# A macaron block with routed experts: the zero fill of the slot table in three large transfers, and matmuls in TensorE's waits

## The reference, cut to what matters

```python
def ffn(x):                               # 16 experts, 2 per token, one shared expert
    probs = softmax(x @ Wr.T + bias)      # (1024, 16)
    val, idx = top_k(probs, 2)
    w = val / (sum(val) + 1e-9)
    y_e = (silu(x @ Wg[e]) * (x @ Wu[e])) @ Wd[e]       # 256 -> 128 -> 256
    routed = sum over the 2 chosen e of w * y_e
    shared = (silu(x @ sWg) * (x @ sWu)) @ sWd
    return routed + shared

def attention(x):                         # 16 heads of 16
    S[i, j] = K[i] . Q[j] * 16 ** -0.5,  -inf for j > i,  decay -(i - j)
    return (softmax(S) @ V) @ o_w.T + o_b

x = x + 0.5 * ffn(layernorm(x))
x = x + attention(layernorm(x))
x = x + 0.5 * ffn(layernorm(x))
```

## Time and profile before

| | |
|---|---|
| median of 3 runs | 366.13 us (365.73 to 367.26) |
| the profiled execution | 365.38 us |
| its span, first to last instruction | 363.6 us |
| mean granted TensorE clock | 0.838 |
| busy share of the span | PE 70%, DVE 70%, ACT 44%, POOL 38% |

### The profile page before, as it was taken

How to read it: one execution, slowest core, us unless ns; L and a number is a source line. 1 busy time by engine, 2 the same in 40 slices (tenths; PEclk the granted TensorE clock), 3 DMA queues, 4 the chain that set the end, 5 groups by cost and what they waited for, 6 DMA issues and landing times.

```text
span 363.6 us, 6430 instructions
## 1 busy us (share of the span) xinstructions
PE 255.2 (70%) x1856; PEld 194.3 (53%) x1856; DVE 254.5 (70%) x839; ACT 160.9 (44%) x411; POOL 136.6 (38%) x212
## 2 busy tenths in 40 slices
PE   1713562999991289679899989898619419999910
PEld 1512551999980169324344444466418309999800
DVE  5673498588883987798688888556676406888716
ACT  3344671455553145315465666756142104656500
POOL 7003884288886014272000000000007732888830
PEclk9966595799997569955999999999867957999965
DMA  5999963655502405863333322000002243555127
GB/s 171 269 182 344 336 237 113 220 157 156 168 23 66 166 0 154 244 183 77 89 87 89 83 52 46 1 2 0 3 0 72 104 134 112 167 154 174 39 78 268
DMA packets 33871, 45.63 MB, mean 125 GB/s; under 512 B 5869, under 2 KB 27419, under 8 KB 33838
## 3 DMA queue, kind: packets, MB, share of 16 engines
q1 hardware_dynamic: 29246, 36.25, 35.4%
q0 software_dynamic: 4592, 8.98, 7.3%
HBM read 27.99 MB, written 20.61 MB: 134 GB/s over the span
## 4 chain that ended last, share of the span: by engine, by line
PE 30%; DMA 19%; POOL 17%; DVE 11%; issue 10%; SPq 8%; ACT 3%; POOLq 0%; DVEq 0%
PE bank L299 18%; POOL slots_x L513 9%; DMA slots_x<-zeros 7%; POOL results L527 6%; DMA stk_q<-parts_d 6%; SPq L412 5%; DVE bank L1261 3%; PE bank L873 3%; PE bank L824 3%; DMA yg<-results 2%; PE bank L886 2%; DMA slots_x<-xn,slot 2%; PE bank L734 2%; POOL yi L521 1%; PE bank L910 1%
## 5 line engine op out<-in xcount | busy, mean ns | idle before, releaser
L527 POOL DMA_INDIRECT results<-ysb,yi x62 | 61.0, 984 | 27.6 <-DVE ysb L1166 14.2
L1261 DVE CUSTOM_DVE_ANT_0 bank<-bank,dec 128x512 f32<-128x512 f32 (+3 forms) x128 | 59.9, 512 | 13.2 <-PE bank L873 12.7
L707 ACT ACTIVATE ct<-bank 128x512 f32<-128x512 f32 (+1 forms) x96 | 46.1, 528 | 39.7 <-PE bank L890 39.1
L513 POOL DMA_INDIRECT slots_x<-xn,slot x32 | 35.5, 1111 | 42.0 <-DMA slots_x<-zeros 19.4
L873 PE MATMUL bank<-stk_q,stk_k 96*128 96x512 bf16 (+3 forms) x128 | 38.6, 343 | 9.1 <-DMA stk_q<-parts_d 4.6
L1127 DVE TENSOR_TENSOR hm<-sg,bank 128x128 f32<-128x128 f32 x78 | 22.3, 287 | 29.7 <-ACT sg L586 29.7
L299 PE MATMUL bank<-wh,xT_h 128*128 x124 | 41.9, 338 | 1.2 <-DVE xT_l L1154 1.2
L624 ACT ACTIVATE xT_h<-bank 128x256 fp32r<-128x256 f32 x62 | 23.8, 384 | 35.8 <-PE bank L824 35.1
L586 ACT ACTIVATE sg<-bank 128x128 f32<-128x128 f32 x78 | 21.6, 276 | 40.2 <-PE bank L299 40.1
L505 POOL COPY xn<-to_row 128x4 int32<-128x4 int32 x8 | 2.4, 301 | 94.0 <-DVE xn L1045 94.0
L824 PE MATMUL bank<-ident,xb 128*128 128x128 f32 x124 | 25.3, 292 | 17.7 <-DMA xb<-slots_x 17.3
(11 more groups left out here) (174 smaller groups left out, 685.9 us busy)
## 6 DMA issues: line engine op xcount, KB each, us to landing
xb<-slots_x SPq DMA_DIRECT2D x62, 128.5 KB
w_raw<-in_experts SPq DMA_DIRECT2D x17, 384.0 KB, 13.5
yg<-results SPq DMA_DIRECT2D x16, 256.0 KB, 4.8
slots_x<-zeros SPq DMA_DIRECT2D x1, 3983.5 KB, 25.6
parts_d<-part SPq DMA_DIRECT2D x6, 384.0 KB, 3.2
stk_k<-parts_d SPq DMA_DIRECT2D x8, 192.0 KB, 3.4
stk_q<-parts_d SPq DMA_DIRECT2D x8, 192.0 KB, 3.7
res<-in_x SPq DMA_DIRECT2D x4, 256.0 KB, 3.5
```

The lines of the kernel that those rows point to most:

```text
L513: pool.indirect_dma_start(slots_x, where, xn[:, t, :], None)\
L527: pool.indirect_dma_start(results, where, ysb[c % RING][:], None, bounds_check=4 * N - 1, oob_is_err=False).then_inc(s_ys[c % RING], 16)
L707: act.activation(ct[n % 6][:, a:b], bank[2 + i][:, 0:b - a], ACT.Exp).then_inc(s_exp, 1)
L1261: dve.tensor_tensor_reduce(s_i, s_i, dec[:, SEQ - w:SEQ], 1.0, NEG, ALU.add, ALU.max, mmax[g % 2][:, n % G * QT + i:n % G * QT + i + 1])\
```

## The change

Four things change.

1. The fill. `zeros` has 11 rows a partition instead of one, and lies in the memory that later holds the `ct` tiles. VectorE writes it as its first work (before: POOL). SP fills the table in three transfers of 11, 10 and 10 rows a partition. The loads of qk_b, v_b and o_b move behind the fill, the shared expert's load stays ahead of it, and r_b and the constant `eps` have semaphores of their own. POOL's scaling of q's bias moves behind the first scatters.
2. The first logits. `logits(0, 0)` runs between the second and third group of transposes and `logits(0, 1)` between the third and the fourth; VectorE's low half of the router weights comes two steps earlier.
3. `keep_busy`: bfloat16 matmuls of 512 columns into a bank whose content isn't used then. Six before the blocks of each `ffn`, when the last group of scatters has landed; seven when the first results have been loaded ahead of attention, and four after each of its first two groups of transposes; four before each of the last two groups of transposes ahead of the second routing.
4. Waits: the scatter waits for three transfers instead of one.

```diff
+        sb("below_zeros", [P, 2 * KT * N], F32, r6)
+        zeros = sb("zeros", [P, 11, XW], F32, r6)
-        zeros = sb("zeros", [P, XW], F32, r2)
...
             sp.dma_start(rw_s[:], r_w).then_inc(s_rws, 16)
-            sp.dma_start(rb[:], r_b.partition_broadcast(P)).then_inc(s_small, 16)
+            sp.dma_start(rb[:], r_b.partition_broadcast(P)).then_inc(s_rb, 16)
+            load_expert(0)
+            rows_of = slots_x.rearrange("(p a) d -> p a d", p=P)
+            sp.wait_ge(s_zero, 2)
+            for a, n in ((0, 11), (11, 10), (21, 10)):
+                sp.dma_start(rows_of[:, a:a + n, :], zeros[:, 0:n, :]).then_inc(s_fill, 16)
             sp.dma_start(qkb[:], qk_b).then_inc(s_small, 16)
             sp.dma_start(vb[:], v_b.partition_broadcast(P)).then_inc(s_small, 16)
             sp.dma_start(ob[:], o_b.partition_broadcast(P)).then_inc(s_small, 16)
-            load_expert(0)
-            sp.wait_ge(s_zero, 3)
-            sp.dma_start(slots_x.rearrange("(p a) d -> p a d", p=P),
-                         zeros[:, None, :].to_broadcast([P, NB, XW])).then_inc(s_fill, 16)
...
-            pool.memset(eps[:], EPS_LN).then_inc(s_zero, 1)
-            pool.memset(zeros[:, 0:D], 0.0).then_inc(s_zero, 1)
-            pool.memset(zeros[:, D:XW].bitcast(I32), NOWHERE).then_inc(s_zero, 1)
+            pool.memset(eps[:], EPS_LN).then_inc(s_eps, 1)
...
-                            pool.wait_ge(s_fill, 16)
+                            pool.wait_ge(s_fill, 48)
...
-            pool.wait_ge(s_small, 64)
+            scatter(0)
+            pool.wait_ge(s_small, 48)
             pool.tensor_scalar(qkb[:, 0, :], qkb[:, 0, :], HD ** -0.5, None, ALU.mult).then_inc(s_qkb, 1)
-            scatter(0)
...
+            def keep_busy(to, n):
+                for _ in range(n):
+                    pe.matmul(to[:], ident_b[:], below_b[:, None, :].to_broadcast([P, QT, P]), start=True, stop=True,
+                              skip_group_check=True)
...
                 pe.wait_ge(s_bex, f + 1)
+                pe.wait_ge(s_sc[3], 8 * NT * (f + 1))
+                keep_busy(bank[5], 6)
...
-            for r in range(NP_):
+            for r in range(2):
                 pe.wait_ge(s_xn, r + 1)
                 turn(0, r)
+            pe.wait_ge(s_const, 2)
             pe.wait_ge(s_rw, 2)
-            pe.wait_ge(s_const, 2)
-            for r in range(NP_):
+            logits(0, 0)
+            pe.wait_ge(s_xn, 3)
+            turn(0, 2)
+            logits(0, 1)
+            pe.wait_ge(s_xn, 4)
+            turn(0, 3)
+            for r in (2, 3):
                 logits(0, r)
...
+            pe.wait_ge(s_yg[0], 16)
+            keep_busy(bank[5], 7)
             for r in range(2):
                 pe.wait_ge(s_xn, NP_ + r + 1)
                 turn(1, r)
+                keep_busy(bank[5], 4)
...
             for r in (2, 3):
+                keep_busy(bank[7], 4)
                 pe.wait_ge(s_xn, 2 * NP_ + r + 1)
                 turn(3, r)
...
-                    dve.wait_ge(s_small, 64)
+                    dve.wait_ge(s_rb, 16)
...
+            dve.memset(zeros[:, :, 0:D], 0.0).then_inc(s_zero, 1)
+            dve.memset(zeros[:, :, D:XW].bitcast(I32), NOWHERE).then_inc(s_zero, 1)
             for r in range(NP_ + 2):
...
-                if r == NP_:
-                    router_low()
                 if r >= 2:
                     turn_low(0, r - 2)
+                if r == 2:
+                    router_low()
```

6 lines of the change are left out of this document (5 added, 1 removed).

## The result

| | median | runs | profiled execution | its span | mean clock |
|---|---|---|---|---|---|
| before | 366.56 us | 365.73 to 367.26 | 365.38 | 363.6 | 0.838 |
| after | 352.69 us | 350.94 to 357.05 | 350.94 | 348.8 | 0.876 |

The ratio is 0.9644, with a 95% interval of 0.9583 to 0.9705: 13.1 us faster, where 5.4 were forecast. Disturbed executions are left out of all ratios here.

What follows compares the result with a forecast made beforehand. The slow zero fill, then scatters beside VectorE's splits, bound the start; TensorE's low clock costs later stretches. 365.38 - 3.3 - 0.6 - 1.1 - 0.4 = 360.0, plus 0.75 for the median: 360.7 us; range 357.6 to 364.3.

Steps and rivals of the forecast that it cites:

- term 1: Start to the end of the first scatters: faster fill and earlier slots end them at 54.5 instead of 57.8, -3.3 us.
- The fill: Zero fill of the slot table at the start: issued at about 4.3, landed at about 17 to 18 us, off the chain.
- The slots: First logits and routing: interleaving logits with transposes gains 0.5 us (0 to 1.6), slots at 27.05.
- The scatters: First scatters on POOL: start at 27.9, are slowed by VectorE's splits and tiles, and end at 54.5 us.
- open 5 us before the rows arrive: Before the first blocks: TensorE's gate, all weights split, opens 5 us before the gathered rows arrive.
- Term 2: Six dummies before both block stages: cost 0.65, gain 1.25 from the higher clock, net -0.6 us (+0.65 to -2.0).
- Term 3: Dummies at the beginning of attention: clock rises about 3 us earlier for Q and K products, -1.1 us (+0.2 to -2.2).
- Term 4: Dummies in the second logits keep the clock high for the last transposes and logits, -0.4 us (+0.6 to -0.9).
- The dummies don't move the clock: Rival for all dummy places: only their ends count as cost; 363.5 us, median 364.3; chance 0.16.
- The fill is no faster: Rival at the start: larger pieces don't speed the fill, landing at 29.9; 362.2 us, median 362.9; chance 0.11.
- slower: Rival at the start: large pieces move near 150 GB/s, fill lands at 33.5; 365.5 to 369.0 us; chance 0.06.
- Everything answers: Rival for the whole kernel: no extra scatter contention, all four stretches at high clock; median say 357.7 us; chance 0.11.

Runs made afterwards that it cites:

- e4: Changed kernel with the table filled as before, in one transfer of 1028-byte rows; 364.28 us, ratio 0.9891 to the kernel before.
- e5: Changed kernel with the loads of experts 11 to 16 issued without waiting for the scatters; 353.75 us, ratio 0.9752 to the kernel before.
- e13: Changed kernel with each wait before the loads of experts 11 to 16 moved one step earlier in the scatters; 354.11 us, ratio 0.9721.
- e7: Changed kernel without the six dummy matmuls before each block stage; 355.18 us, ratio 0.9771 to the kernel before.
- e6: Changed kernel with the six dummies before the blocks placed ahead of the wait for the weights' splits; 353.10 us, ratio 0.9708.
- e12: Changed kernel timed again, unaltered, as reference beside other kernels; 354.71 us, ratio 0.9708 to the kernel before.
- e8: Changed kernel without the 15 dummy matmuls at the beginning of attention; 357.74 us, ratio 0.9851 to the kernel before.
- e17: Kernel before with only the dummy matmuls at the start of attention added; 362.67 us, ratio 0.9949.
- e18: Changed kernel without the eight dummies between the second logits' transposes; 354.76 us, ratio 0.9702 to the kernel before.
- e1: Changed kernel without any of its 35 dummy matmuls, fill and first logits as changed; 359.56 us, ratio 0.9792 to the kernel before.
- e2: Kernel before with the 35 dummy matmuls alone added; 362.03 us, ratio 0.9841.

## Why the prediction was wrong

The direction was right, and both halves of the change work; the gain was undersized by more than half (5.4 us forecast, 10.7 to 13.1 measured). Two steps failed. The first is the overlap of scatters and weight splits in term 1: the last scatter was put at 54.5 us and ended at 49.90, and the weights, not the rows, open the blocks. The second is attention behind the Q and K products, which the sum put at nothing and which was 3.9 us shorter in the profile. By its own steps:

**The fill: right.** The memset took 2.40 us (taken 3.0, bounds 1.75 to 3.5), the transfers were issued at 4.29 (4.3) and the last landed at 18.8 (17 to 18). e4 shows that the form of the transfers is the cause; that it is the size of the pieces, as the prediction had it, is not shown. The first scatter came at 26.31 instead of 27.9, because of the next step.

**The slots: mis-sized.** -2.1 us instead of -0.5. I counted gaps and priced the logits at the lower level. With transposes and logits in one nearly unbroken stretch the level rose at 12.99 instead of 17.36 (at 12.0 to 14.9 in all profiles with the new order, 14.8 to 17.4 with the old), and the last two groups of logits ran at 0.28 instead of 0.41 us a matmul.

**The scatters: the failed step of term 1.** "The scatters meet it fully" was wrong in its size: I had VectorE's 21.65 us unbroken from 30.1 on. In fact the loads of experts 11 to 16 hang on the scatters, which I had read in the code for the change and not in this sum; VectorE idled 3.00 us, scatters went undisturbed meanwhile, and the sixteen took 23.59 us, not 26.6. Last scatter 49.90, not 54.5; last split 53.24, not 51.8. So the weights, and not the rows, open the blocks, the reverse of "open 5 us before the rows arrive". e5 and e13 show that the forecast's picture (splits at 51.8, scatters at 54.5) is what the kernel does when the gates are loosened: 50.5 and 53.9.

**Term 2, dummies before the blocks: mis-sized on both sides.** The cost in the first stage was not 0.3 us but 2.0 (e7), since they wait for the weights and nothing is left to hide them; in the second 0.4, as said. Of the return I took half of a capped 2.6 us for both stages; it was 2.1 in the first and 1.4 in the second. The reason for halving was a misread row: of the "4.97 of 13.6 us" the first 9.7 us lie ahead of the first block's transposes. From 300.1 to 304.0 TensorE was busy 3.83 of 3.90 us, from 61.7 to 68.5 it was 6.15 of 6.80, and at the higher level after the change 7.50 of 7.60. The uncapped 4.0 us would have been near the 3.5 measured. Net -0.1 and -1.0 in these two profiles, up to -2.1 by the medians of e6 and e7, for -0.6 forecast; with the six stages of other kernels in which the dummies brought nothing, about 0 on average. "I take half" had no such chance in it.

**Term 3: right in its place, blind beyond it.** -1.1 up to the last QK product, as forecast. Attention behind it gave 3.9 more, for which the prediction had no term: 2.4 of them are the level's rise 8.7 us nearer to the first exponential. The trace of before had this, the level low until 174.4, but I only looked for stretches next to an edit. About 1.6 of the 3.9 are gone in e12, the same kernel, so that much is luck. How much of the rest the change brought stays open (e8, e17).

**Term 4: right.** -0.7 for -0.4; e18's median can't tell it from nothing.

**The rivals.** "The dummies don't move the clock" is refuted as a rule by e1, e2 and the sixteen short stages, though it is what happened in six others. "The fill is no faster" and "slower" are refuted by 434 GB/s; the fall of the rate that the first of them pointed to is real, but only in the fill in rows. "Everything answers" (357.7) came nearest and was still too slow: it lacked the weights' gate, the slots and attention. The range's lower end was built from bounds of four terms, and none covered a stage that the change doesn't touch.

## What to carry to other kernels

When a transfer leaves the path, don't only move what stood behind it: list every wait that is tied to that work's progress (here loads gated on scatters), since it decides which of two parallel chains ends last. TensorE's clock level is a cost of stages, not of instructions: look at every stretch at the lower level in the trace of before, and try matmuls directly ahead of the first real one, where they cost least; followed by 4 us of idleness they were worth nothing, and directly ahead they worked in 16 of 22 stages. Count such an effect over all the profiles that you have before you believe one pair. And repeat the changed kernel before dividing its gain, because one kernel spread over 5 us. Last, check what a busy share was divided by: a stretch that begins before the work makes an engine look idle.

## What the runs showed of the hardware

- A fill of DRAM with pieces of 10 to 11 KB a partition ran at 404 to 434 GB/s, with pieces of 1028 bytes at 176 to 183 in its middle. The fill in rows began at 336 GB/s and fell to 146 (kernel before, stretches of 2 us); stores of 1024-byte pieces elsewhere took 46 ns a piece.
- Small loads behind the large fill held SP for 1.1 us each; behind the fill in rows, the first held it for 11.0 (13.0 in e4).
- A VectorE memset of 2816 floats a partition took 2.40 us, 0.85 ns an element, where the two-input subtraction takes 1.24.
- A scatter on POOL took 0.96 us alone and up to 2.16 (kernel before) beside VectorE's subtractions of two SBUF tiles; beside memsets its median was 0.964.
- Six 512-column matmuls directly ahead of a block stage had TensorE's higher level there 0.3 to 1.7 us into it in 16 stages, and 5.7 to 6.8 us in 6 others; without them directly ahead it came 4.7 to 7.7 us into it in all 12.
- TensorE's level changed at different points in executions of one kernel: behind the first exponential by 2.4 us in one and 8.2 in another.
